# Patch embedding, attention and soft mixture of experts on one core: token tiles of 128 and one joint stage for queries, keys and values

## The reference, cut to what matters

```
p = layernorm(patches) * g1 + b1            # 1152 x 768
h = layernorm(p @ W_tok) * g2 + b2          # 1152 x 192
q, k, v = h @ W_qkv                         # 8 heads of 24, each 192 wide
a = softmax((q/|q|).T @ (k/|k|) * temp)     # per image and head: 24 x 24, norms over the 36 tokens
h = layernorm(h + (a @ v.T).T @ W_proj + b_proj)
# soft mixture of experts: 8 experts of 4 slots, per image
D = softmax(logits over tokens); C = softmax(logits over the 32 slots)
Y = C @ (gelu((D.T @ h/|h|) @ W_down + b_down) @ W_up + b_up)
out = layernorm(h + Y)
```

## Time and profile before

| | |
|---|---|
| median of 3 runs | 133.83 us (132.72 to 134.02) |
| time of the profiled execution | 132.76 us |
| its span, first to last instruction | 131.0 us |
| PE busy | 113.6 us, 87% |
| DVE busy | 86.9 us, 66% |
| ACT busy | 71.9 us, 55% |
| POOL busy | 66.4 us, 51% |
| mean granted TensorE clock | 0.968 |

### The profile page before, as it was taken

One profiled execution on the slowest core, in us unless ns is written; L12 is line 12 of the kernel. 1 busy time (PEld: TensorE's weight loads), 2 busy tenths in 40 slices (PEclk: granted clock), 3 DMA queues, 4 the chain that ended last, 5 costly groups with the idle time before them and its releaser, 6 DMA issues.

```text
span 131.0 us, 4847 instructions
## 1 busy us (share of the span) xinstructions
PE 113.6 (87%) x1779; PEld 92.6 (71%) x1779; DVE 86.9 (66%) x380; ACT 71.9 (55%) x236; POOL 66.4 (51%) x158
## 2 busy tenths in 40 slices
PE   0099999799999999999999999999995988899930
PEld 0099996769787689768787776989773776677610
DVE  0126883929758386737992796899998344488870
ACT  3000023435467661467758856957779768836672
POOL 8600366636667186998953293555423300215780
PEclk9999999999999999999999999999999596899997
DMA  2999998795410000000000000000000000000223
GB/s 11 334 313 285 276 324 315 305 316 165 125 46 8 0 8 0 5 0 5 3 5 5 0 5 5 0 10 0 5 0 5 0 3 0 0 5 25 72 71 104
DMA packets 7678, 10.35 MB, mean 79 GB/s; under 512 B 2056, under 2 KB 5032, under 8 KB 7656
## 3 DMA queue, kind: packets, MB, share of 16 engines
q1 hardware_dynamic: 7656, 10.06, 25.0%
HBM read 9.17 MB, written 0.88 MB: 77 GB/s over the span
## 4 chain that ended last, share of the span: by engine, by line
PE 68%; ACT 10%; DVE 7%; issue 5%; POOL 4%; DMA 3%; SPq 1%; POOLq 1%; DVEq 0%; ACTq 0%
PE ps L410 11%; PE ps L434 11%; PE ps L480 7%; PE ps L581 5%; ACT hb L1043 5%; PE ps L502 5%; PE ps L493 4%; DMA wt<-in_w_tok 3%; PE ps L465 3%; PE ps L398 3%; PE ps L525 3%; PE ps L452 2%; PE ps L548 2%; ACT L1043 2%; PE ps L421 2%
## 5 line engine op out<-in xcount | busy, mean ns | idle before, releaser
L410 PE MATMUL ps<-wc,xT 128*108 128x192 f32 (+1 forms) x132 | 23.2, 328 | 0.1
L410 PEld LDWEIGHTS ps<-wc,xT 128*108 128x108 f32 (+1 forms) x132 | 20.8, 170 | 0.9 <-issue 0.4
L947 ACT ACTIVATE hT<-ps,b,g 96x108 f32<-96x108 f32 (+1 forms) x22 | 8.3, 431 | 20.8 <-PE ps L421 20.8
L434 PE MATMUL ps<-wqk,hT 96*108 96x384 f32 (+1 forms) x44 | 16.5, 497 | 0.0
L971 ACT ACTIVATE km<-ps,imgsel 108x192 f32<-108x192 f32 (+1 forms) x32 | 11.1, 417 | 6.1 <-PE ps L434 6.1
L581 PE MATMUL ps<-wu,hb 128*96 128x192 f32 (+1 forms) x44 | 11.0, 385 | 2.0 <-ACT hb L1043 2.0
L480 PE MATMUL ps<-hT,wv 96*128 96x108 f32 (+1 forms) x88 | 12.0, 279 | 0.0
L480 PEld LDWEIGHTS ps<-hT,wv 96*128 96x128 f32 x88 | 10.9, 191 | 0.7
L641 DVE BATCH_NORM_STATS2 st<-xs 108x6 f32<-108x384 f32 (+1 forms) x22 | 10.9, 537 | 0.0
L1166 POOL TENSOR_SCALAR var<-mv 108x1 f32<-108x1 f32 (+1 forms) x11 | 2.5, 223 | 15.9 <-DVE mv L873 15.8
L1094 POOL TENSOR_SCALAR var<-mv 108x1 f32<-108x1 f32 (+1 forms) x11 | 2.4, 222 | 14.5 <-DVE mv L647 14.0
(11 more groups left out here) (107 smaller groups left out, 302.3 us busy)
## 6 DMA issues: line engine op xcount, KB each, us to landing
xT<-in_x_t SPq DMA_DIRECT2D x10, 324.0 KB, 7.7
xs<-in_x SPq DMA_DIRECT2D x10, 324.0 KB
out<-o SPq DMA_DIRECT2D x10, 81.0 KB
wt<-in_w_tok SPq DMA_DIRECT2D x1, 576.0 KB, 4.2
wqk<-in_w_qk SPq DMA_DIRECT2D x1, 288.0 KB, 8.2
xT<-in_x_t SPq DMA_DIRECT2D x1, 216.0 KB, 6.8
xs<-in_x SPq DMA_DIRECT2D x1, 216.0 KB
wv<-in_w_v SPq DMA_DIRECT2D x1, 192.0 KB, 8.6
```

What stands on the lines that cost most here:

```text
L410: mm = pe.matmul(tokp(g), xT[:, o + kc * n:o + (kc + 1) * n], wc[:, kc, :], start=kc == 0, stop=kc == KC - 1)
L434: mm = pe.matmul(qkp(g), hT[:, f, t0:t0 + tokens(g)], wqk[:, f, :, :, :].rearrange("p j h d -> p (j h d)"), start=f == 0, stop=f == 1)
L947: ins = act.activation(hT[:, f, t0:t0 + tokens(g)], htp(g)[:, f, :], ACT.Identity, bias=b2[:, f:f + 1], scale=g2[:, f:f + 1])
```

## The change: what it does

- Tokens are embedded in 9 tiles `t` of 128 tokens in place of 11 groups of 108 or 72. All steps from `x_stats` to `take_h` and `keep_h_offset` go by tiles. The turned weights and patches are laid out anew in memory.
- The normed tile is kept as h0, 128 x (192 + 64): features 128 to 191 stand in it twice, so that one turn of its second half puts these 64 features on partitions 0 to 63 and again on 64 to 127. `ln2_norm` has a second, 64 wide instruction for that.
- `qk` and `values` become one stage `qkv(g)`: first 128 features for queries and keys (384 columns) and for both halves of the values, on the whole array; then the other 64 features, queries and keys in two matmuls of 192 columns on array rows 0 to 63, and values in two matmuls on rows 64 to 127, in turns. It waits for all three readers of the group before.
- The tiles are cut back into groups by 19 transfers, h0 to z, inside the core's memory (`regroup`), issued by SyncE; `residual(g)` waits for them.
- The start forms the column means as a matmul of g1/768 (broadcast) with W_tok itself, which comes in two halves; VectorE then makes each of the six slices of wc in one instruction.
- The experts' hidden stage has two batches, groups 0 to 7 and 8 to 10, both in PSUM bank 0.
- All engines' lists are in a new order.

```diff
-HB = ((0, 4), (4, 8), (8, NG))
+HB = ((0, 8), (8, NG))
...
+            def regroup(g):
+                sp.wait_ge(r_ready, last_tile(g) + 1)
+                for t, p, q, n in pieces(g):
+                    sp.dma_start(z[q:q + n, g, :], h0[p:p + n, t, 0:D]).then_inc(h0_in[g], 16)
...
+            def column_means():
+                pe.wait_ge(gs1_ready, 1)
+                for kc in range(KC):
+                    if kc % (KC // 2) == 0:
+                        pe.wait_ge(wtok_in[kc // (KC // 2)], 16)
+                    mm = pe.matmul(csp(), gs1[:, kc:kc + 1].broadcast_to([128, 128]), wt[:, kc, :],
+                                   start=kc == 0, stop=kc == KC - 1)
+                mm.then_inc(csp_ready, 1)
...
+            def turn_h(t):
+                pe.wait_ge(n_ready, t + 1)
...
+                if t >= 1:
+                    pe.wait_ge(hT_ready, t)
+                for f in range(2):
+                    mm = pe.transpose(htp(t)[:, f, :], h0[:, t, f * 128:(f + 1) * 128], ident[:, :])
+                mm.then_inc(htp_ready, 1)
...
+            def qkv(g):
+                n, t0 = tokens(g), g * GI * TOK
+                main, rest = hT[:, 0, t0:t0 + n], hT[:, 1, t0:t0 + n]
+                pe.wait_ge(hT_ready, last_tile(g) + 1)
...
                 if g >= 1:
                     pe.wait_ge(sq_ready, g)
                     pe.wait_ge(qk_ready, g)
-                for f in range(2):
-                    mm = pe.matmul(qkp(g), hT[:, f, t0:t0 + tokens(g)],
-                                   wqk[:, f, :, :, :].rearrange("p j h d -> p (j h d)"),
-                                   start=f == 0, stop=f == 1)
-                mm.then_inc(qkp_ready, 1)
+                    pe.wait_ge(v_ready, g)
+                pe.matmul(qkp(g), main, wqk[:, :], start=True, stop=False)
+                for m in range(2):
+                    pe.matmul(vp(g)[:, m, :], wv[:, m, :], main, start=m == 0, stop=False)
+                for m in range(2):
+                    pe.matmul(qkp(g)[:, m * D:(m + 1) * D], rest[0:R], wrest[0:R, m * D:(m + 1) * D],
+                              start=False, stop=m == 1, tile_position=(0, 0))
+                    mm = pe.matmul(vp(g)[:, m, :], wrest[R:2 * R, m * 128:(m + 1) * 128], rest[R:2 * R],
+                                   start=False, stop=m == 1, tile_position=(R, 0))
+                mm.then_inc(qkvp_ready, 1)
...
             def token_weights():
+                dve.wait_ge(csp_ready, 1)
                 for kc in range(KC):
-                    dve.tensor_scalar(wg[:, kc, :], wt[:, kc, :], g1[:, kc:kc + 1], None,
-                                      ALU.mult).then_inc(wg_ready, 1)
-                dve.wait_ge(wg_ready, KC)
-                dve.wait_ge(csp_ready, 1)
-                dve.tensor_tensor(wc[:, :, :], wg[:, :, :], csp().unsqueeze(1).broadcast_to([128, KC, D]),
-                                  ALU.subtract).then_inc(wc_ready, 1)
+                    dve.scalar_tensor_tensor(wc[:, kc, :], wt[:, kc, :], gb1[:, 0, kc:kc + 1], csp(),
+                                             ALU.mult, ALU.subtract).then_inc(wc_ready, 1)
...
+                dve.tensor_scalar(h0[:, t, D:D + R], y1[:, t % NB, 128:D], mv2[:, t, 0:1], rstd2[:, t:t + 1],
+                                  ALU.subtract, ALU.mult)
+                dve.tensor_scalar(h0[:, t, 0:D], y1[:, t % NB, :], mv2[:, t, 0:1], rstd2[:, t:t + 1],
+                                  ALU.subtract, ALU.mult).then_inc(n_ready, 1)
```

More of the change, by code:

```diff
@@ L36 @@
 NG = (B + GI - 1) // GI
+NT = NTOK // 128
 F = D // 2
+R = D - 128
 NE, NP = 8, 4
@@ L53, in tokens, with pieces, last_tile, build @@
     return images(g) * TOK
-def build(nc, x, x_t, w_tok, ln1_g, ln1_b, ln2_g, ln2_b, g2col, b2col, w_qk, w_v, w_proj, b_proj, temp, slots, scale,
+def pieces(g):
+    a, e, out = g * GI * TOK, g * GI * TOK + tokens(g), []
+    while a < e:
+        n = min(e, (a // 128 + 1) * 128) - a
+        out.append((a // 128, a % 128, a - g * GI * TOK, n))
+        a += n
+    return out
+def last_tile(g):
+    return pieces(g)[-1][0]
+def build(nc, x, x_t, w_tok, ln1_gb, ln2_g, ln2_b, g2col, b2col, w_qk, w_v, w_rest, w_proj, b_proj, temp, slots, scale,
           w_down, b_down, w_up, b_up, ident_h, imgsel_h, negmask_h, out):
@@ L380, in _ @@
+            regroup(9); regroup(10); store(0); store(1); store(2); store(3); store(4); store(5)
+            store(6); store(7); store(8); store(9); store(10)
             for i in range(NQ):
@@ L401, in token @@
[L401 to L410 removed]
+            def token(t):
+                o = t * 128 * KC
+                pe.wait_ge(xT_in[t], 16)
+                if t >= 2:
+                    pe.wait_ge(y1_ready, t - 1)
+                for kc in range(KC):
+                    if t == 0:
+                        pe.wait_ge(wc_ready, kc + 1)
+                    mm = pe.matmul(tokp(t), xT[:, o + kc * 128:o + (kc + 1) * 128], wc[:, kc, :],
@@ L595, in combine @@
                           start=True, stop=True).then_inc(yop_ready, 1)
-            column_means(); offset(); token(0); token(1); token(2); turn_h(0); token(3); qk(0)
-            values(0); turn_h(1); token(4); norms(0); qk(1); gram(0); token(5); turn_h(2); token(6)
-            norms(1); qk(2); turn_h(3); gram(1); values(1); token(7); norms(2); qk(3); mix(0); turn_h(4)
-            values(2); project(0); gram(2); norms(3); turn_h(5); qk(4); mix(1); token(8); norms(4)
-            gram(3); values(3); token(9); turn_h(6); gram(4); project(1); qk(5); token(10); mix(2)
@@ L608, in _ @@
-            turn_l(3); gram(10); values(9); logits(4); mix(8); turn_xn(5); turn_l(4); slot_in(1)
-            values(10); turn_dc(2); project(8); logits(5); slot_in(2); turn_xn(6); turn_l(5); turn_dc(3)
-            mix(9); logits(6); slot_in(3); turn_l(6); turn_xn(7); turn_dc(4); project(9); logits(7)
-            slot_in(4); turn_l(7); turn_xn(8); turn_dc(5); hidden(0); mix(10); logits(8); project(10)
-            turn_l(8); slot_in(5); slot_out(0); turn_dc(6); slot_out(1); turn_xn(9); slot_in(6)
@@ new lines, in _ @@
+            token(3); gram(0); norms(0); qkv(1); token(4); turn_h(2); norms(1); token(5); turn_h(3)
+            qkv(2); gram(1); token(6); mix(0); qkv(3); gram(2); norms(2); turn_h(4); project(0)
+            norms(3); token(7); gram(3); qkv(4); token(8); turn_h(5); norms(4); mix(1); qkv(5)
+            project(1); gram(4); turn_h(6); norms(5); mix(2); qkv(6); project(2); turn_h(7); gram(5)
+            mix(3); norms(6); qkv(7); project(3); gram(6); turn_h(8); norms(7); mix(4); qkv(8)
+            turn_xn(0); project(4); turn_xn(1); logits(0); mix(5); gram(7); norms(8); turn_l(0)
@@ new lines, in _ @@
+            project(5); qkv(9); logits(1); mix(6); turn_xn(2); turn_dc(0); gram(8); turn_l(1)
+            project(6); slot_in(0); logits(2); mix(7); turn_xn(3); norms(9); turn_l(2); turn_dc(1)
+            project(7); gram(9); logits(3); turn_xn(4); slot_in(1); turn_l(3); qkv(10); logits(4)
+            turn_dc(2); mix(8); turn_xn(5); turn_l(4); slot_in(2); project(8); turn_xn(6); logits(5)
+            norms(10); turn_dc(3); turn_l(5); gram(10); mix(9); slot_in(3); logits(6); turn_dc(4)
+            project(9); turn_xn(7); slot_in(4); turn_l(6); turn_dc(5); mix(10); logits(7); slot_in(5)
```

570 lines of the change are left out of this document (256 added, 314 removed).

## The result

| | before | after, first measurement | after, measured again |
|---|---|---|---|
| median | 133.52 us (132.72 to 134.02, 4 runs) | 127.83 us (126.53 to 129.16, 4 runs) | 126.81 us (125.99 to 128.67, 6 runs) |
| ratio, 95% interval | | 0.950 [0.941, 0.960] | 0.946 [0.941, 0.951] |
| profiled execution, its span | 132.76, 131.0 | 128.50, 126.5 | 127.14, 125.0 |

The change is about 5% faster; 126.7 was predicted. Both changed columns are the same kernel. The ratios leave out executions more than 1.5% above the fastest of their kernel, and each stands against the kernel before as measured beside it (133.52 us for the first, 133.90 for the second).

What follows compares the result with a forecast made beforehand. TensorE was taken to bound the long middle (busy 88.97 of 90.34 us). From 132.76 us, -1.2 - 3.9 - 3.5 + 0.7 + 1.3 = -6.6 gave 126.2; half of 1.07 added made 126.7, range 121.5 to 132.

Steps and rivals of the forecast that it cites:

- start: Up to the first turns: tokens begin 1.7 us sooner, 1.4 idle added, a 0.9 wait gone; 1.2 us gained, between 0 and 2.5.
- tokens: Token embedding on TensorE: 132 instructions become 108, 24 fewer at 0.1625 us each, 3.9 us less.
- joint stage: Queries, keys and values per group: row halves overlap, 1.98 us for 2.27, saving 3.5 us; bounds 5.5 saved to 3.7 lost.
- end: Experts' gelu waits in two batches: idle 3.6 us against 2.6, less 0.3 for one hidden stage; 0.7 lost, between -1 and +4.
- cover: Other engines keeping up with a shorter TensorE, VectorE already at 85%: 1.3 us given back, between 0 and 4.
- The 0.18 us for entering the divided array: Joint stage: one handover from the whole array to small tiles, 0.18 us a group, counted within its 1.98 us.
- The wait for all three readers and the regrouping: `qkv(g+1)` waiting for ScalarE's readers, and residuals for 19 transfers: both costed at nothing; slower rival from the readers, 136.7 us, 0.08.
- I expect the same low level behind it, no dearer: After the longer wait for the first gelu: TensorE's clock falls to the same low level as before, at no extra cost.

Runs made afterwards that it cites:

- two sets of transfers: Changed kernel with each regrouping transfer preceded by another like it into an unread tile, residuals waiting for both: 126.72 us, 0.948 of the kernel before.
- taking one link out: Changed kernel plus eight useless matmuls in TensorE's end waits, and slot_in of groups 4 to 7 in PSUM bank 1: 124.15 us, 0.931 of the kernel before.
- plain 64-row matmuls: Changed kernel with the other 64 features' products as 64-row matmuls without array places, value weights also on rows 0 to 63: 131.14 us, 0.981 of the kernel before.
- fillers and slots apart: Changed kernel plus eight useless matmuls before slot_out(0), and slot_in of groups 4 to 7 in PSUM bank 1: 124.15 us, 0.931 of the kernel before.

## Why the prediction was right, point by point

The predicted time was met for mostly the reasons given, and in part by luck, since terms that were off by more than a microsecond cancel. The table sets the terms of the sum beside what the runs showed (second profile, where nothing else is said). Times of stages are added up from the start of each to the start of what follows, without idle time.

| term | predicted | measured |
|---|---|---|
| start | -1.2 | -2.1 first work, +0.4 idle up to 60 us: -1.7 (first profile -1.3); the old start put back costs 1.5 to 2.1 |
| tokens | -3.9 | 108 instructions for 132; 18.5 us for 22.2: -3.6 |
| joint stage | -3.5, 1.98 us each | 25.7 us before; first profile 22.5: -3.2; second 23.5: -2.3 |
| end | +0.7 | idle 3.38 against 4.04, and one hidden stage less (0.3): -1.0 |
| cover | +1.3 | +1.9 of idle time between 60 us and `hidden(0)` |

- **Start: right.** Column means from 4.83 (4.6 said), tokens from 10.33 (10.4), first turn at 15.74 (15.7 to 16.0) after 1.35 idle (1.4), and the wait for the second turn is gone.
- **Joint stage: mechanism right, size near.** The halves overlap. Three things were off. The sum took 0.32 us a group where its own 2.27 - 1.98 is 0.29; eleven times that is 3.2, which is what the first profile shows. The 0.18 us for entering the divided array is about half too high: the entry shows as 0.08 to 0.09 us, with a place given or not, and the last instruction of the rest takes 0.25 us too (19.71 to 19.96). With other small costs (values 0.13 us each and not 0.12) this makes the rest 0.82 us (19.14 to 19.96) where 0.65 was reckoned, so the 1.98 came out at 1.99. And in the second profile three joint stages took 2.33 to 2.42 us. The Trainium skill, "TensorEngine Tiling (Array Packing)", section "Key Properties", says that a change of tiling mode drains TensorE; the 0.08 us at the entry agrees with that in kind, and no run here separates a drain from other causes. Its other rule, that tiles multiply in parallel, the trace bears out.
- **The wait for all three readers and the regrouping: right at nothing.** No such wait shows in the changed kernel; two sets of transfers bring one of 0.5 us and don't change the time.
- **Cover: the term that was mis-sized**, 1.3 said, and 1.9 us of idle found. The reasoning had VectorE's work some 3.5 us less; its busy time fell by 0.4 (86.9 to 86.5). The patches' statistics take 2.1 us less in nine tiles than in eleven groups, but `ln2_norm` with two instructions a tile takes 1.7 more. VectorE is busy 88% from 60 us to `hidden(0)` (85% before). The waits there name ScalarE's `xt` (1.0 us) and `cT` (0.4), beside the 0.5 that nothing explains, and slots follow each other every 2.20 us, the pace of a chain of short steps from TensorE to ScalarE and VectorE and back; taking one link out made it 1.99.
- **Busy time: 2.0 us that the sum doesn't have.** 113.53 less 3.9, 3.5 and 0.3 makes 105.8, and 107.86 was measured. Tokens account for 0.3 and the joint stages of that profile for 1.2. Another 1.8 lies in stages that the change left alone: `project` 0.5, `logits` and `combine` 0.4 each, `turn_dc` and `norms` about 0.25 each, with the same number of instructions. `slot_out` and some others took less, 1.3 together. The low clock falls on other stages than before, which can be part of it; the rest stays open.
- **End: sum and cause right, the price of the clock left out.** About 2.9 us of waiting was foreseen before the first `slot_out`, and 1.81 + 1.03 = 2.84 came. Two thirds of it is booked under group 10's norm on VectorE, but gelu ends last and would have held TensorE as long. In the second profile the waits for gelu, with that one, are 3.24 us against 2.67 before, +0.6 where +1.0 was said; what the sum didn't have is 1.2 us of other small idle times that went, most of it waits for `cT` (0.54), `xt` (0.41) and `yT` (0.17). And "I expect the same low level behind it, no dearer" held only for part of the executions: 7.0 us at the low level in one profile, as before (6.9), 10.2 in the other. Taking the low level away gains 2.2 us, the largest gain of any experiment here, and I had it in the sum only as something that cancels.

Errors cancel: the start came out 0.5 us better than said and the end 1.7, cover and busy time together 2.6 worse.

## What to carry to other kernels

Two products over 64 features each, on the two row halves of the array, took 0.82 us together here where one after the other took 1.24; so where two products have a contraction of 192, each can be cut as 128 + 64, with their 64s side by side. It paid here by the overlap alone: without it the joint stage was slower than the separate ones. When TensorE's work shrinks, follow its waits with the lists of the other engines, since the next limit here was a chain of short steps through three engines. Where two waits follow each other with little work between them, ask which releaser comes last: here `xn` took two thirds of the waiting and gelu set its end. After any wait of TensorE of one or two microseconds, compare the duration of the same instruction before and behind it; if it has doubled, work that nobody needs, put into the wait, may be the cheapest gain, but only if no later wait undoes it.

## What the runs showed of the hardware that wasn't expected

- **Row halves start out of list order.** With four instructions on rows 0 to 63 listed ahead of them, the ones on rows 64 to 127 started 0.02 us after the first of the four (18.93 and 18.91). The stage's signal still kept the order. It hangs on the last instruction of the values, whose modelled end in the changed kernel's trace is 19.84; it came at 20.06, 0.03 us after the last instruction of queries and keys (20.03). In the version with plain 64-row matmuls, where the values end last, it came 0.01 us after them (20.31 and 20.32). The Trainium skill, "PSUM — Partial Sum Buffer", section "Engine vs sequencer instructions", says that matmuls start and complete in program order; by these rows the start doesn't keep to it between row halves, and the signal of completion does.
- **Useless matmuls give time back.** Eight of them, 2.6 us of work in waits of 1.8 and 1.0 us, held the granted clock at 1.00 where it was 0.50 to 0.67 between 100 and 110 us, and gained 2.2 us.
- **Joint stages of groups 6 to 9 vary without a cause.** TensorE stood 0.74 us at the values of group 9 (near 69 us) for nothing that the profile names, 0.5 to 0.8 in other versions and not at all with the plain 64-row matmuls. In groups 6 to 8 the stage took 2.05 to 2.08 us in the first profile and 2.36, 2.42 and 2.33 in the second, of the same kernel; with fillers and slots apart the one of group 7 took 2.70. One execution can differ from another by a microsecond in this way, so gains of that size are better read from one stage than from the whole time. That stays open.
